# Results of the early epochs kept in item order: ScalarE stores them, GpSimd gathers each tile's rows

## What is computed

```
x = x + segment_sum(layernorm(x)[src] * edge_weight, dst) @ W.T + b      # 212500 edges, sorted by dst
probs = softmax(layernorm(x) @ gate_w + gate_b)                          # 8 experts
top2_vals, top2_idx = top_k(probs, 2)
x = x + sum over the two chosen experts e of probs[e] * (gelu(layernorm(x) @ W1[e] + b1[e]) @ W2[e] + b2[e])
```

## Time and profile before

| | before |
|---|---|
| median of 3 runs | 2654.87 us (2648.48 to 2655.98) |
| the profiled execution: its time | 2653.09 us |
| its span | 2651.2 us |
| PE busy | 2118.5 us, 80% |
| DVE busy | 1464.6 us, 55% |
| ACT busy | 664.3 us, 25% |
| POOL busy | 1819.5 us, 69% |
| DMA | 652.64 MB, mean 246 GB/s |

### The profile page before, as it was taken

How to read it: one execution, slowest core, us unless ns; L and a number is a source line. 1 busy time by engine, 2 the same in 40 slices (tenths; PEclk the granted TensorE clock), 3 DMA queues, 4 the chain that set the end, 5 groups by cost and what they waited for, 6 DMA issues and landing times.

```text
span 2651.2 us, 47128 instructions
## 1 busy us (share of the span) xinstructions
PE 2118.5 (80%) x11356; PEld 1664.7 (63%) x11357; DVE 1464.6 (55%) x6118; ACT 664.3 (25%) x1932; POOL 1819.5 (69%) x1905
## 2 busy tenths in 40 slices
PE   4666776698689699987788789799898887996595
PEld 3444454476477577765566566577777766775485
DVE  7888454465365364464466375364556565574243
ACT  2332121122122123222122122123232222322232
POOL 7666777777777777777777777777777776770021
PEclk8767898899899899998889899899999988998798
DMA  8766846867758768858879868869788887985596
GB/s 290 242 199 213 250 141 190 262 205 240 238 187 256 251 205 283 287 175 275 279 223 315 269 210 273 257 190 319 256 259 284 286 281 248 322 267 165 168 369 220
DMA packets 304874, 652.64 MB, mean 246 GB/s; under 512 B 61364, under 2 KB 196182, under 8 KB 291926
## 3 DMA queue, kind: packets, MB, share of 16 engines
q1 hardware_dynamic: 171812, 356.59, 40.0%
q0 software_dynamic: 90624, 247.58, 30.7%
q10 hardware_dynamic: 42162, 45.37, 4.9%
HBM read 548.25 MB, written 210.23 MB: 286 GB/s over the span
## 4 chain that ended last, share of the span: by engine, by line
PE 27%; POOL 24%; DVE 14%; issue 13%; DMA 11%; SPq 9%; DVEq 1%; ACT 1%; ACTq 0%; POOLq 0%
POOL rows L450 22%; PE bank L783 9%; PE bank L876 8%; SPq L568 6%; PE bank L860 6%; DMA slots<-stage 5%; POOL results L477 2%; DMA results<-y_sb,result_i 2%; DVE spread L1237 2%; DMA rows<-xhat,src_t 1%; DVE bn L1216 1%; DMA xi<-slots 1%; DMA stage<-sorted_x 1%; PE bank L803 1%; PE bank L811 1%
## 5 line engine op out<-in xcount | busy, mean ns | idle before, releaser
L450 POOL DMA_INDIRECT rows<-xhat,src_t x1488 | 1425.9, 958 | 468.4 <-issue 448.5
L783 PE MATMUL bank<-rows,spread 128*80 128x256 f32 x3328 | 890.1, 428 | 222.7 <-DMA rows<-xhat,src_t 151.2
L783 PEld LDWEIGHTS bank<-rows,spread 128*80 128x80 f32 x3328 | 557.7, 171 | 517.5 <-issue 187.6
L876 PE MATMUL bank<-w,hT 128*128 x1792 | 457.5, 401 | 53.0 <-DVE y_sb L1448 33.0
L860 PEld LDWEIGHTS bank<-xiT,w 128*128 128x128 f32 x3584 | 442.8, 195 | 32.5 <-DMA w<-in_w 8.7
L860 PE MATMUL bank<-xiT,w 128*128 128x128 f32 x3584 | 446.8, 279 | 12.2 <-DMA w<-in_w 7.0
L876 PEld LDWEIGHTS bank<-w,hT 128*128 128x128 f32 x1792 | 339.5, 200 | 111.2 <-issue 69.5
L1250 DVE TENSOR_TENSOR acc<-acc,bank 128x160 f32 x208 | 66.9, 322 | 616.8 <-PE bank L773 557.0
L1054 ACT ACTIVATE hT<-bank,b1T 128x128 f32<-128x128 f32 x896 | 255.8, 368 | 597.2 <-PE bank L860 523.7
L477 POOL DMA_INDIRECT results<-y_sb,result_i x224 | 222.6, 994 | 259.7 <-DVE y_sb L1448 206.4
L1237 DVE TENSOR_SCALAR spread<-iota_w,dst_rel,wgt 128x80 f32<-128x80 f32 x1488 | 365.2, 339 | 0.1
(11 more groups left out here) (175 smaller groups left out, 1694.7 us busy)
## 6 DMA issues: line engine op xcount, KB each, us to landing
w<-in_w SPq DMA_DIRECT2D x224, 512.0 KB
slots<-stage SPq DMA_DIRECT2D x784, 136.0 KB
xi<-slots SPq DMA_DIRECT2D x224, 136.0 KB, 4.7
stage<-sorted_x ACTq DMA_DIRECT2D x98, 272.0 KB
rows<-xhat,src_t POOLq DMA_INDIRECT x1488
got<-results SPq DMA_DIRECT2D x73, 256.0 KB, 5.6
x_t<-in_x SPq DMA_DIRECT2D x97, 128.0 KB
x_d<-x_t ACTq DMA_DIRECT2D x97, 128.0 KB
```

Of the source, the lines that this page charges most:

```text
L450: pool.indirect_dma_start(rows[q][:, c, :], None, x if g < RAW else xhat, bass.IndirectOffsetOnAxis(ap=src_t[:, g * CG + c:g * CG + c + 1] ...
L783: done = nc.tensor.matmul(B_SUM[0:W, 0:D], spread[g % 2][:, c, :], rows[q][:, c, :], start=c == 0, stop=c == CG - 1)
L876: done = nc.tensor.matmul(bank[:, 0:D], hT[i % 2][:, j, :], w2[:, bass.ds(e, 1), j, :].rearrange("p o f -> p (o f)"), start=j == 0, stop=j ...
```

## The change

For the items of the first three epochs (FIRST_LATE = 189 of them) ACT stores `y_sb` as it is, 128 rows in a block of their own, with a plain DMA to `yq` in DRAM. There is no scatter and no copy of target rows for them. `place` on DVE also keeps for every node and choice which queue block and which row of it the node is in, in 10 more instructions for each of the 12 parts below tile 84. At the end of an epoch SP writes the list of items to DRAM and reads it back to all partitions. For each of the 84 tiles DVE then finds the item of each node's block and makes two index columns (`index_results`, 6 instructions). POOL gathers the tile's 2 x 128 result rows with two indirect DMAs, in place of the plain load by SP. The 35 items of the last epoch are scattered as before.

The planner changes with it: the early items are `queued` for ACT one turn after `down`, before the first Gelu of the turn; the index of a tile is made one per turn (4 per turn in the tail), and its gathers follow 3 turns later (1 in the tail). The turns in which tiles are combined stay within one turn of those before, the tail's batches included.

```diff
+FIRST_LATE = FIRST_ITEM[-2]
...
-            t.results += [s[0] for s in back.steps if s[0] >= 0 and s[0] not in result_at]
+            t.results += [s[0] for s in back.steps if s[0] >= FIRST_LATE and s[0] not in result_at]
         if turns:
             t.combines, t.stores = turns[-1].fetches, turns[-1].combines
+            t.queued = [s[0] for s in turns[-1].steps if 0 <= s[0] < FIRST_LATE]
...
+        while index_next < LATE and len(t.index) < (1 if busy else BATCH):
+            if not result_at.get(FIRST_ITEM[EPOCH_OF[PART_OF[index_next]] + 1] - 1, tau) < tau:
+                break
+            index_at[index_next] = tau
+            t.index.append(index_next)
+            index_next += 1
...
-            if not result_at.get(FIRST_ITEM[m + 1] - 1, tau) < tau - (2 if busy else 0):
+            if not index_at.get(fetch_next, tau) < tau - (2 if busy else 0):
                 break
...
+    yq = nc.dram_tensor("yq", (FIRST_LATE * P, D), F32, kind="Internal").ap()
+    lists = nc.dram_tensor("lists", (FIRST_LATE,), F32, kind="Internal").ap()
...
+            def gather_results(t, to, done):              # POOL
+                if t in EPOCH_TILES:
+                    results_done(t)
+                pool.wait_ge(indexed, t + 1)
+                for c in range(2):
+                    pool.indirect_dma_start(to[:, c, :], None, yq[0:FIRST_ITEM[EPOCH_OF[PART_OF[t]] + 1] * P], bass.IndirectOffsetOnAxis(ap=gather_i[:, t, c:c + 1], axis=0)).then_inc(done, 16)
...
                     for i in t.results:
                         scatter_result(i)
+                    if t.batch >= 0:
+                        gather_batch(plan, t, fast, first_batched)
+                    elif t.busy:
+                        for u in t.fetches:
+                            if u >= CB:
+                                pool.wait_ge(res_ready, u - CB + 1)
+                            gather_results(u, got[u % CB], got_in[u % CB])
...
-                sp.dma_start(got[b][0:n], result_pairs[t * P:t * P + n]).then_inc(got_in[b], 16)
...
-                    sp.dma_start(pairs[j][0:n], result_pairs[u * P:u * P + n]).then_inc(batch_in[q], 16)
...
+            def store_y(i):                               # ACT, ahead of gelu in the turn
+                act.wait_ge(y_ready, i + 1)
+                act.dma_start(yq[i * P:(i + 1) * P], y_sb[i % YB][:]).then_inc(y_kept[i % YB], 16)
...
+                if t0 < LATE:                             # DVE, in place, ahead of sort offsets and masks
+                    qp = queue_pos[:, 0:n, :]
+                    then(nc.vector.tensor_tensor(qp, ps, B_GATE[:, 0:n * NX].rearrange("p (t e) -> p t e", e=NX), op=ALU.add))
+                    for c, mk in enumerate((m1, m2)):
+                        then(nc.vector.tensor_tensor(cd, mk, qp, op=ALU.mult))
+                        then(nc.vector.tensor_reduce(queue_row[:, 0:n, c], cd, axis=AX.X, op=ALU.add))
+                    ri, pi = row_i[:, 0:n, :], part_i[:, 0:n, :]
+                    then(nc.vector.tensor_copy(ri, queue_row[:, 0:n, :]))
+                    then(nc.vector.tensor_scalar(pi, ri, P.bit_length() - 1, None, op0=ALU.arith_shift_right))
+                    then(nc.vector.tensor_copy(block_of[:, t0:t1, :], pi))
+                    then(nc.vector.tensor_scalar(pi, ri, P - 1, None, op0=ALU.bitwise_and))
+                    then(nc.vector.tensor_copy(row_of[:, t0:t1, :], pi))
...
                 if i >= YB:
-                    dve.wait_ge(y_out[i % YB], 16 * (i // YB))
+                    if i - YB < FIRST_LATE:
+                        dve.wait_ge(y_kept[i % YB], block_moves(i % YB) + 16 * (i // YB))
+                    else:
+                        dve.wait_ge(y_out[i % YB], late_stores(i % YB, i))
                 dve.wait_ge(y_summed, i + 1)
-                nc.vector.tensor_copy(result_i[i % YB][:], xi[i % XI][:, bass.ds(e + C_ID, 1)]).then_inc(result_i_ready, 1)
+                if i >= FIRST_LATE:
+                    nc.vector.tensor_copy(result_i[i % YB][:], xi[i % XI][:, bass.ds(e + C_ID, 1)]).then_inc(result_i_ready, 1)
...
+            def index_results(t):                         # DVE, behind combine in the turn
+                m = EPOCH_OF[PART_OF[t]]
+                if t in EPOCH_TILES:
+                    dve.wait_ge(list_moved, 32 * (m + 1))
+                here = slice(FIRST_ITEM[m], FIRST_ITEM[m + 1])
+                hit = item_hit[:, 0:EPOCH_ITEMS[m]]
+                for c in range(2):
+                    then(nc.vector.scalar_tensor_tensor(hit, item_all[:, here], block_of[:, t, c:c + 1], item_row[:, here],
+                                                        op0=ALU.is_equal, op1=ALU.mult))
+                    then(nc.vector.tensor_reduce(item_of[:, c:c + 1], hit, axis=AX.X, op=ALU.add))
+                then(nc.vector.tensor_tensor(item_of[:], item_of[:], row_of[:, t, :], op=ALU.add))
+                nc.vector.tensor_copy(gather_i[:, t, :], item_of[:]).then_inc(indexed, 1)
+                dve.wait_ge(indexed, t + 1)
```

More of the change, by code:

```diff
@@ L140 @@
     steps: list = field(default_factory=list)
+    index: list = field(default_factory=list)
+    list_store: int = -1
+    list_load: int = -1
+    queued: list = field(default_factory=list)
     results: list = field(default_factory=list)
@@ L232, in plan @@
         for back in turns if not busy else turns[:-1]:
-            t.results += [s[0] for s in back.steps if s[0] >= 0 and s[0] not in result_at]
+            t.results += [s[0] for s in back.steps if s[0] >= FIRST_LATE and s[0] not in result_at]
         if turns:
             t.combines, t.stores = turns[-1].fetches, turns[-1].combines
+            t.queued = [s[0] for s in turns[-1].steps if 0 <= s[0] < FIRST_LATE]
         stored += len(t.stores)
-        for i in t.results:
+        for i in t.queued + t.results:
             result_at[i] = tau
+        for k, at in listed_at.items():
+            if ends_epoch(k) and EPOCH_OF[k] < NE - 1:
+                if at == tau - 1:
+                    t.list_store = EPOCH_OF[k]
+                if at == tau - 2:
+                    t.list_load = EPOCH_OF[k]
+        if t.listing >= 0:
+            listed_at[t.listing] = tau
+        while index_next < LATE and len(t.index) < (1 if busy else BATCH):
[4 more added lines that the diff above has]
+            index_next += 1
         all_sent = sent_at.get(NK - 1, tau) < tau
@@ L595, in load_xi, with load_node_rows @@
                 sp.dma_start(w1[:, i % W1B], w1_in[:, bass.ds(e, 1)].rearrange("p o k h -> p (o k) h")).then_inc(w1_in_sem[i % W1B], 16)
-            def load_results(t, first):
+            def load_node_rows(t):
                 n, b = valid_rows(t), t % CB
[L599 to L602, removed]
                 sp.wait_ge(x1_out[t % XB], 16 * (t // XB + 1))
@@ L645, in finish_late @@
                 for b in range(YB):
-                    sp.wait_ge(y_out[b], 16 * len(range(b, NI, YB)))
+                    sp.wait_ge(y_out[b], late_stores(b, NI))
                 last = max(t.batch for t in plan)
@@ L671, in load_ahead, with store_list, load_list, move_lists @@
                     load_rows(b)
+            def store_list(m):
+                sp.wait_ge(listed, [k for k in range(NK) if EPOCH_OF[k] == m][-1] + 1)
+                sp.dma_start(lists[FIRST_ITEM[m]:FIRST_ITEM[m + 1]], item_f[0, FIRST_ITEM[m]:FIRST_ITEM[m + 1]]).then_inc(list_moved, 16)
+            def load_list(m):
+                sp.wait_ge(list_moved, 32 * m + 16)
+                sp.dma_start(item_all[:, FIRST_ITEM[m]:FIRST_ITEM[m + 1]], lists[FIRST_ITEM[m]:FIRST_ITEM[m + 1]].partition_broadcast(P)).then_inc(list_moved, 16)
+            def move_lists(t):
+                if t.list_store >= 0:
+                    store_list(t.list_store)
+                if t.list_load >= 0:
+                    load_list(t.list_load)
             def send(u):
@@ L697, in tail_turn @@
                     load_kept(u)
+                move_lists(t)
                 if t.late:
@@ L1067, in tail_turn @@
                     exponent(t.choose)
+                for i in t.queued:
+                    store_y(i)
                 for _, b, c, _ in t.steps:
@@ L1500, in tail_turn @@
                         combine(u)
+                for u in t.index:
+                    index_results(u)
                 if t.listing >= 0:
```

40 lines of the change are left out of this document (31 added, 9 removed).

## The result

The changed kernel takes 2686.5 us (median of 4 runs, 2683.7 to 2696.1), the kernel before 2653.1 us beside it; ratio 1.0124, 95% interval 1.0099 to 1.0149. I had predicted 2622 us, in a range of 2572 to 2660. The sum had -31.6 us; +33.4 us came.

What follows compares the result with a forecast made beforehand. POOL was taken as the bound, with PE a near second. Terms -38.6 (POOL), -8 (scatter waits), +8 (place), +5 (index) and +2 (tail) summed to -31.6 us against 2653.1 us, giving 2622 us, range 2572 to 2660.

Steps and rivals of the forecast that it cites:

- the second bound: PE, a near bound behind POOL: 90 to 92% busy in dense stretches, 95% taken as reachable in mixed ones.
- POOL's ledger with the scatter waits, -46.6 us: POOL's scatters removed and gathers added, -38.6 us, with -8 us for DVE's results no longer waiting for scatters.
- -75.7 us: Scatters leaving POOL in the first half of each epoch's life: 44.2 us where PE has room, 31.5 us capped by PE.
- +29.5 us: POOL in 1160 to 1590: 30 tiles' gathers add 75.0 us, 35 scatters leave, 45.5 us.
- +7.6 us: POOL in 2000 to 2386: +26.7 us from gathers against scatters, less 19 us swallowed by POOL's lead and waits for PE.
- DVE's scatter waits, -8: DVE's 79.9 us of waits for scatters to land go; bounds 0 and -26, taken as -8 us.
- place, +8: DVE's ten more instructions in place, 2.4 us in 12 turns, 29 us; bounds 0 and +29, taken as +8.
- index_results, +5: Six DVE instructions, 1.44 us in 62 busy turns, 89 us; bounds 0 and +89, taken as +5.
- DVE's additions reach PE: Rival: DVE's additions delay results that PE's down waits for; full price 118 us, at half 2668 us; chance 0.11.
- Nothing arrives: Rival: PE sets the long-run pace, or transfers are the bound; 2653 us, within 10 us of before; chance 0.13.
- The last turns, +2: Tail: none of POOL's saving, four indices cost DVE 5.8 us per turn; bounds -2 and +12, taken as +2.
- The sign of being wrong: POOL's idle pieces grow without PE being busy, and PE's waits for y_sb rise from 33 us by tens.

Runs made afterwards that it cites:

- e12: e1 with SyncE issuing two more one-row copies per tile, whose data nobody uses; 2679.8 us, 1.0109 of the kernel before.
- e13: The kernel before with SyncE issuing the same two more one-row copies per tile, whose data nobody uses; 2694.7 us, 1.0161 of the kernel before.
- e2: e1 with POOL gathering each early tile's two halves by one fixed index (wrong rows), without DVE's additions; 2649.0 us, 0.9982 of the kernel before.
- e1: Changed kernel with ACT's stores alone: no index, place additions, list moves or POOL result gathers; SyncE loads other rows; 2588.0 us, 0.9748 of the kernel before.
- e5: e1 with DVE's additions in place as well, no index, lists or gathers; 2625.8 us, 0.9900 of the kernel before.
- e3: e1 with DVE's additions in place, list moves and index kept, rows by plain loads; 2659.1 us, 1.0011 of the kernel before.
- e6: e1 with DVE's index and the list moves, but nothing added in place; 2623.3 us, 0.9896 of the kernel before.
- e14: e1 with ACT issuing four of eight run copies last in its turn, a part's last tile excepted; 3337.6 us, where the kernel before took 3539.
- e15: Changed kernel with spread gathers, later place additions, three-tile index, and e14's division of copies; 3540.8 us, 1.0006 of the kernel before on that chip.
- e1b: e1 run again, unchanged, on another chip where the kernel before took 3610.9 us; 3408.4 us, 0.9460 of it.
- e14b: e14 run again, unchanged, on another chip where the kernel before took 3610.9 us; 3398.4 us, 0.9425 of it.

## Why the prediction was wrong

*What bounds the kernel before: half of it.* That POOL has no free time is right, and an indirect DMA costs it 1.25 to 1.30 us. That PE is "the second bound", and the only one behind POOL, is the step that fails: there stands a third chain, from the sorted stage over SyncE's eight copies, 6 us in a row, to the load of the next items. The page of the kernel before had it in its chain of waits, and in the chain inside 620 to 890 it has a larger share (27%) than POOL's gathers (19%). I let SyncE go with "SP loses 84 loads" and a 0, and took POOL's queue and PE's 95% as the only two limits. What the runs show in its place: with POOL relieved, each us added to SyncE's queue costs 0.80 us (e12), before 0.39 (e13).

*POOL's ledger with the scatter waits, -46.6 us.* Here 44 us of the 65 between forecast and result are lost: e2, which holds just these terms, is at -2.6 us. Its sums say where. Of the "-75.7 us" of relief the ledger has 52.2 up to 1160, and 21 us came; from 1590 to 2000 it has 23.5 us, and 6 came. DVE's additions aren't to blame for that: e2 has none, and gained the same 21 and 6 us, and e1, which has no gathers either, gained 38 matmuls up to 1160, 27 us. In 620 to 890 neither POOL nor PE was the bound, so the relief of 22 scatters had nowhere to go. PE did come near the cap of 95% where it is dense (93% in 890 to 1160).

"+29.5 us" for the stretch in which epoch 0 is combined looks right, since 28 us came in the kernel after, but that is luck: in e2 it was 16 us, and the other 12 came from DVE's additions, which the term didn't hold. The +7.6 us behind 2000 agree with e2's 5.

*DVE's scatter waits, -8.* They went (no scatter is issued before 2400 us), but no run has this term alone.

*place, +8: mis-sized.* It is 38 us in e5, which the upper bound of 29 us meets within the noise. The argument for +8, that in half of the places PE waits and POOL is the bound in a part of those, was made from the kernel before. That the price depends on POOL shows in two pairs: place and index together cost 71 us where POOL has no gathers of results (e3 over e1) and 37 where it has them (the changed kernel over e2). What they would cost in the kernel before was not run.

*index_results, +5: mis-sized.* Ahead of the last turns it cost 17 us in e6, the moves of the lists included, to which I had given 0. PE's few waits for `y_sb` were read as room on DVE. They did fall, from 33.0 to 22.2 us, and still the index cost. Which of the instructions behind it on DVE carries the delay, and how much of it is SyncE's wait for the lists, is not shown.

*Both beside POOL's gathers.* From e2 to the changed kernel they cost 37 us: predicted were 15 with the last turns, so this is the other 22 us. The rival "DVE's additions reach PE" had a full price of 118 us and half of it as its case; its sign was right, but its path (PE waiting for `y_sb`) was seen in the last turns alone; in busy turns PE waited for masks instead. "Nothing arrives", 2653 us, is where e2 stands. But neither PE's pace nor the transfers hold it there: e1, with the same matmuls and 652.60 MB in place of 652.64, takes 64 us less than the kernel before. (The DMA shares that I gave for this rival as 0.74 to 0.82 are 0.74 to 0.84 in the earlier trace rows, and 1.06 in the tail.)

*The last turns, +2: mis-sized.* They cost 17 us, nearly all of it the index (e6): for four tiles 6 us of DVE ahead of the results that PE waits for. I had that price and let it lie beside PE.

*ACT's stores, 0:* nothing in the runs speaks against it, and none has it alone. *What would show it.* The last gathers were to end "near 2340 us"; they ended at 2396.0 us, with 58 indirect DMAs fewer ahead of them (182 less 124, not 59). The sign of being wrong came by half: POOL's idle time grew without PE being busy, but PE's waits for `y_sb` fell.

*The rule that spoke against the change.* Moving the stores off POOL's queue gained 64 us by itself (e1), and SyncE's own time to issue is on the path at 0.80 us per us (e12). e1's stores are also plain ones and no longer scatters, which no run separates. The Trainium skill (DMA: Bandwidth & Descriptors, Issuing engines are not separate DMA queues) calls the sequencer time saved usually small beside the DMA; by that rule e1 would have stood at 2652 us. The measurement decides, for this kernel.

## What to carry to other kernels

When a load is taken off the bounding engine, don't stop at the second bound: go through the chain of waits, stretch by stretch, and ask of each queue how much of it would be left on the path. The price of an edit on another engine is to be taken at the new bound, not read from waits under the old one; a dose of idle work on one queue, with one run for each kernel, measures that price. And work that comes with a change belongs into turns that another engine bounds: the same gathers, spread over twice the turns, were 27 us cheaper.

## What the hardware showed that I had not expected

A copy from DRAM to DRAM holds SyncE longer than a load to SBUF: the one-row copies of e12 have a median of 572 ns, the copies of a tile's runs, whose addresses come from registers, 521, the load of an item's rows 333 (in each row: count, then minimum/median/maximum of one issue). First a row of e12, then two of e1:

```profile
L626 SPq DMA_DIRECT2D unused<-in_x x196: 517/572/1157, 261.2 to 2530.0; - x196
```

```profile
L625 SPq DMA_DIRECT2D slots<-stage x784: 520/521/1338, 260.8 to 2442.6; - x196
L649 SPq DMA_DIRECT2D xi<-slots x224: 331/333/561, 323.0 to 2540.0; - x112
```

Size has little to do with it: 1 KB for the 572 ns, 136 KB for the 521. And on two chips the kernel before took 3539 and 3611 us instead of 2652, while a gather held POOL as long as ever (953 ns in e14 and e15, 957 in e1). From e1 to e1b, the same kernel, the mean granted clock is 0.83 in place of 0.91 and a matmul of the sums takes 453 ns in place of 418; PE is busy 256 us longer, of 815 us that the span grows. The profile names another core or an unknown queue for 14 and 17% of the chain of e1b and e14b. Why, I can't say.
